# A graph network block on one core: places of a counting sort carried on in PSUM in place of column scans, padding spread over several rows, and the gather list turned by two groups

## What is computed

```
z    = concat([x[src], x[dst], edge_attr]) @ W.T + b          # per edge, 256 wide
z    = batch_norm(z, over all edges)
msg  = sigmoid(z[:, :H]) * softplus(z[:, H:])
agg  = zeros_like(x).at[src].add(msg)
x1   = layernorm(x + x + agg)
sums = segment_sum(x1[src], dst);  cnt = segment_sum(1, dst)
gain = tanh(norm(x1 - sums / max(cnt, 1)))
h    = x1 + 0.2 * (relu(x1 @ W1 + b1) @ W2 + b2) * gain
out  = layernorm(x1 + layernorm(h))
```

## Time and profile before

| what | value |
|---|---|
| time, median of 3 executions | 3955.68 us (3945.11 to 3955.88) |
| the profiled execution, span | 5481.6 us |
| stage 1, counting and source chain | 0 to 380 us of the profile |
| stage 1, list loop | 380 to 1749 us |
| stage 2 | 1749 to 3300 us |
| stage 3 | 3300 to 4249 us |
| stage 4 | 4249 to 5407 us |
| stage 5 | 5407 to 5482 us |

### The profile page before, as it was taken

The page is one execution under the profiler, slowest core; times in us unless marked ns, Lnnn a source line. Parts: engine busy times, 40 slices in busy tenths (PEclk is TensorE's granted clock), DMA queues, the critical chain, the costliest instruction groups (busy, mean ns, idle before and its releaser), DMA issues. The chain is left out here.

```text
span 5481.6 us, 84513 instructions
## 1 busy us (share of the span) xinstructions
PE 3436.3 (63%) x18854; PEld 2395.6 (44%) x18855; DVE 2979.6 (54%) x7781; ACT 2242.8 (41%) x6113; POOL 2626.3 (48%) x2634
## 2 busy tenths in 40 slices
PE   6745666666656888888888885661175555455542
PEld 2312222222223666666666664551165445445542
DVE  7975555555655333333333337971198555455547
ACT  1405555555654444444444448971197000000002
POOL 3775444444553555555555550077600544545542
PEclk8957777778877888888888887885587777777766
DMA  5322222122221666656666575463443221222213
GB/s 166 110 88 67 60 65 63 59 61 65 61 68 56 191 190 186 195 186 188 188 191 188 184 173 222 169 241 114 130 194 87 58 49 47 53 53 53 56 41 39
DMA packets 314711, 638.06 MB, mean 116 GB/s; under 512 B 54382, under 2 KB 188567, under 8 KB 306551
## 3 DMA queue, kind: packets, MB, share of 16 engines
q0 software_dynamic: 99440, 246.85, 16.9%
q1 hardware_dynamic: 172984, 266.76, 15.7%
q10 hardware_dynamic: 42192, 123.38, 6.1%
HBM read 424.53 MB, written 212.24 MB: 116 GB/s over the span
## 5 line engine op out<-in xcount | busy, mean ns | idle before, releaser
L367 POOL DMA_INDIRECT rec_d<-arena x830 | 887.8, 1070 | 815.8 <-issue 520.7
L853 POOL DMA_INDIRECT arena<-b_tab,arena x880 | 839.2, 954 | 730.4 <-DVE arena L874 405.8
L767 PE MATMUL psum<-arena 128*128 128x440 f16 x3360 | 776.5, 390 | 369.5 <-DVE arena L626 140.8
L626 DVE TENSOR_SCALAR arena<-iota_t,arena 128x880 f16<-128x880 f16 x840 | 516.1, 664 | 545.9 <-remote 320.5
L461 ACT ACTIVATE arena<-arena 128x128 f16<-128x128 f16 x1680 | 568.5, 388 | 469.9 <-remote 333.1
L767 PEld LDWEIGHTS psum<-arena 128*128 128x128 f16 x3360 | 344.2, 106 | 803.5 <-DVE arena L626 322.1
L1569 PE MATMUL psum<-arena,x_sb 128*128 128x129 f32 x2304 | 398.3, 347 | 454.2 <-DVE x_sb L1456 320.9
L964 PE MATMUL psum<-weT,arena 128*128 128x256 f32 x1760 | 627.6, 443 | 31.9 <-DVE arena L874 21.9
L1448 DVE TENSOR_TENSOR arena<-psum,arena 128x258 f32 x880 | 375.3, 426 | 476.9 <-remote 282.2
L1569 PEld LDWEIGHTS psum<-arena,x_sb 128*128 128x128 f32 x2304 | 375.7, 257 | 480.4 <-issue 192.3
L1255 POOL DMA_INDIRECT arena<-x_tab,arena x304 | 299.9, 987 | 556.1 <-DMA x_tab<-arena 295.9
(11 more groups left out here) (251 smaller groups left out, 5920.5 us busy)
## 6 DMA issues: line engine op xcount, KB each, us to landing
z_d<-arena ACTq DMA_DIRECT2D x220, 512.0 KB
arena<-z_d SPq DMA_DIRECT2D x44, 2560.0 KB
arena<-rec_d SPq DMA_DIRECT2D x220, 260.0 KB
arena<-in_edge_attr SPq DMA_DIRECT2D x83, 640.0 KB
arena<-early_d SPq DMA_DIRECT2D x34, 516.0 KB
arena<-b_tab,arena POOLq DMA_INDIRECT x880
rec_d<-arena POOLq DMA_INDIRECT x831
early_d<-arena POOLq DMA_DIRECT2D x9, 1032.0 KB
```

The lines of the kernel that those rows point to most:

```text
L367: nc.gpsimd.indirect_dma_start(rec_rows, bass.IndirectOffsetOnAxis(e_idx[:, s, k:k + 1], 0), e_buf[:, s, k, :], None).then_inc(s_es[s], 16)
L626: nc.vector.tensor_scalar(hot_tile[:, s, :].rearrange("p (a b) -> p a b", b=TILE_RUN), iota_t[:, :, 0:TILE_RUN], tile_f[:, bass.ds(t, 1)], ...
L767: last = nc.tensor.matmul(bank(4 + 2 * k + h)[:, 0:HALF], hot_lane[:, s, k, :], hot_tile[:, s, h * HALF:(h + 1) * HALF], start=start, stop ...
L853: nc.gpsimd.indirect_dma_start(bg[:, s, k, :], None, b_tab, bass.IndirectOffsetOnAxis(rec[:, s, k, H:H + 1].bitcast(I32), 0)).then_inc(s_b ...
```

## The change

There are three edits.

**Places carried on.** For each of the two chains, one bank of PSUM now holds, for every key and column, the place at which the next edge of that column goes. It starts from the counts (`chain_starts`: one scan, two more operations, once for each chain). In a step PE adds the ranks inside the column (`ranks`, one matmul with `tribig`), DVE reads the bank, and then PE adds the rest of the column's count (`move_on`: two matmuls, `restb` and `identb`), so that the bank is ready for the next step. The scans and the running sums of every step are gone. The destination's loop body now holds two batches.

**Padding over several rows.** The padding records' destination is `N_NODES` + (lane mod 16). In the second list an empty slot points to a row of its own lane (`PAD_ROW` + lane), 128 zeroed rows.

**List turned.** The second list is turned by `LAST_FIRST` = 2 groups (16 tiles): its last two groups come first. `EARLY` is 36. The first two groups are gathered at the start of stage 3 (when they are empty, for which the wait is on `s_end`), the other 34 as before. So there are 74 direct groups, 18 rounds and two direct groups behind them.

```diff
-EARLY, EARLY_BLOCKS, EARLY_TILES = 34, 16, 300
+EARLY, EARLY_BLOCKS, EARLY_TILES = 36, 16, 300
+LAST_FIRST = 2
+END_TILES = LAST_FIRST * G
...
-                def sum_columns(dest, hots):
-                    return nc.vector.tensor_tensor_scan(dest, not_first[:, 0:dest.shape[1]], hots, 0.0, ALU.mult, ALU.add)
+                def chain_starts(places, counted, n):
+
+                    upto, first = chain[:, 0, 0:n * G_IN], chain[:, 1, 0:n * G_IN]
+                    after(nc.vector.tensor_tensor_scan(upto, not_first[:, 0:n * G_IN], counted, 0.0, ALU.mult, ALU.add))
+                    after(nc.vector.tensor_tensor(first, upto, counted, ALU.subtract))
+                    after(nc.vector.scalar_tensor_tensor(by_col(places), tstart[:, 0:n].unsqueeze(2).broadcast_to([P, n, G_IN]), float(P), by_col(first),
+                                                         ALU.mult, ALU.add))
...
+                after(nc.vector.tensor_scalar(lane_row, lane, 15, None, ALU.bitwise_and))
+                after(nc.vector.tensor_scalar(pad_dst, lane_row, float(N_NODES), None, ALU.add))
...
                     if b + 2 < NB:
                         hot(hot_s[:, (b + 2) % 4, :], hi_s, b + 2).then_inc(s_hr, 1)
-                        dve.wait_ge(s_hr, b + 3)
-                        sum_columns(upto_s[:, (b + 2) % 3, :], hot_s[:, (b + 2) % 4, :]).then_inc(s_up, 1)
...
-                    if b + 3 < NB:
-                        run_src(b + 3)
                     dve.wait_ge(s_rg, b + 1)
-                    after(nc.vector.tensor_reduce(pos10, by_col(bank(b % 2)[:, 0:HB]).rearrange("p b c -> p c b"), op=ALU.max, axis=AX_X))
-                    nc.vector.tensor_scalar(p_i, pos10, -BIG, None, ALU.add).then_inc(s_rd, 1)
+                    nc.vector.tensor_reduce(pos10, by_col(CHAIN_S).rearrange("p b c -> p c b"), op=ALU.max, axis=AX_X).then_inc(s_rd, 1)
                     dve.wait_ge(s_rd, b + 1)
+                    after(nc.vector.tensor_scalar(p_i, pos10, -BIG, None, ALU.add))
...
-                def next_hot(b):
-                    nc.vector.tensor_tensor(run_d, run_d, by_col(upto_d)[:, :, G_IN - 1], ALU.add).then_inc(s_card, 1)
-                    hot(hot_d, hi_d, b).then_inc(s_hd, 1)
-                    dve.wait_ge(s_hd, b + 1)
-                    sum_columns(upto_d, hot_d).then_inc(s_upd, 1)
+                def next_hot(b, s):
+                    hot(hot_d[:, s, :], hi_d, b).then_inc(s_hd, 1)
...
-                after(nc.vector.tensor_scalar(l1_idx[:, 0:G * EARLY], l1_idx[:, 0:G * EARLY], early_key, None, ALU.add))
+                padded = l_words[:, 0:SLOTS]
+                after(nc.vector.tensor_scalar(padded[:, END_TILES:G * EARLY], l1_loc[:, END_TILES:G * EARLY], 0.0, early_key, ALU.is_gt, ALU.mult))
+                after(nc.vector.tensor_tensor(l1_idx[:, END_TILES:G * EARLY], l1_idx[:, END_TILES:G * EARLY], padded[:, END_TILES:G * EARLY], ALU.add))
+                after(nc.vector.tensor_scalar(padded, l1_loc[:], 0.0, pad_row, ALU.is_equal, ALU.mult))
+                after(nc.vector.tensor_tensor(l1_idx[:], l1_idx[:], padded, ALU.max))
...
+                def ranks(places, hots):
+
+                    return nc.tensor.matmul(places, tribig, hots, start=False, stop=False, skip_group_check=True)
+
+                def move_on(places, hots):
+
+                    nc.tensor.matmul(places, restb, hots, start=False, stop=False, skip_group_check=True)
+                    nc.tensor.matmul(places, identb[:], hots, start=False, stop=False, skip_group_check=True)
...
                     pe.wait_ge(s_hr, b + 1)
-                    pe.wait_ge(s_up, b + 1)
-                    if b >= 2:
-                        pe.wait_ge(s_rd, b - 1)
-                    ranks(bank(b % 2)[:, 0:HB], hot_s[:, b % 4, :], upto_s[:, b % 3, :])
+                    ranks(CHAIN_S, hot_s[:, b % 4, :]).then_inc(s_rg, 1)
                     if ab < BLOCKS:
                         less(ab, 0)
-                    pe.wait_ge(s_run, b + 1)
-                    before(bank(b % 2)[:, 0:HB], run_s[:, b % 4, :]).then_inc(s_rg, 1)
+                    pe.wait_ge(s_rd, b + 1)
+                    move_on(CHAIN_S, hot_s[:, b % 4, :])
...
                 for g in range(EARLY):
+                    if g == LAST_FIRST:
+                        pool.wait_ge(s_xs, ready)
+                        settle(pool, s_turn)
```

More of the change, by code:

```diff
@@ L222, in build @@
         hot_tile = tmp([HOTS, SLOTS], F16)
-        upto_s = tmp([3, HB], BF16)
+        tmp([3 * SLOTS - HOTS * SLOTS // 2], F32)
+        chain = arena[:, list_at:list_at + 2 * HK].rearrange("p (a n) -> p a n", a=2)
         l_words = arena[:, list_at:list_at + 3 * SLOTS]
@@ L267, in build @@
         COUNT_S, COUNT_D = bank(3)[:, 0:HB], bank(7)[:, 0:HK]
+        CHAIN_S, CHAIN_D = bank(0)[:, 0:HB], bank(1)[:, 0:HK]
         def by_col(v):
@@ L524, in tile_pairs @@
                 def tile_pairs():
-                    blocks_of(tile_id, blkf, KEYS)
+                    after(nc.vector.tensor_scalar(tile_in_list, tile_id, float(END_TILES), float(SLOTS), ALU.is_lt, ALU.mult))
+                    after(nc.vector.scalar_tensor_tensor(tile_in_list, tile_id, -float(END_TILES), tile_in_list, ALU.add, ALU.add))
+                    blocks_of(tile_in_list, blkf, KEYS)
                     after(nc.vector.tensor_scalar(blkf4, blkf, float(PAIRS), -float(PAIRS), ALU.is_ge, ALU.mult))
@@ L608, in _ @@
                 block_tiles(COUNT_D, KEYS)
-                nc.vector.tensor_copy(run_d, tstart).then_inc(s_card, 1)
-                hot(hot_d, hi_d, 0).then_inc(s_hd, 1)
-                dve.wait_ge(s_hd, 1)
-                sum_columns(upto_d, hot_d).then_inc(s_upd, 1)
+                chain_starts(CHAIN_D, COUNT_D, KEYS)
+                hot(hot_d[:, 0, :], hi_d, 0).then_inc(s_hd, 1)
                 tile_pairs()
@@ L654, in _ @@
                 places(1)
-                with dve.Fori(2, NB) as it:
-                    next_hot(it)
-                    dve.wait_ge(s_card, 5 * it)
-                    for k in range(G_IN):
-                        hots((it - 1) * G_IN + k, k % HOTS, it * G_IN + (k + 1 - HOTS - G_IN))
-                    places(it)
-                dve.wait_ge(s_card, 5 * NB)
+                with dve.Fori(1, NB // 2) as it:
+                    for h in range(2):
+                        b = 2 * it + h
+                        next_hot(b, h)
+                        dve.wait_ge(s_card, 4 * b)
+                        for k in range(G_IN):
+                            hots((b - 1) * G_IN + k, k % HOTS, b * G_IN + (k + 1 - HOTS - G_IN))
+                        places(b)
+                dve.wait_ge(s_card, 4 * NB)
                 for k in range(G_IN):
@@ L726, in _ @@
                     count_src(b + 4)
-                def ranks(region, hots, upto):
-                    nc.tensor.matmul(region, tribig, hots, start=True, stop=False, skip_group_check=True)
-                    nc.tensor.matmul(region, onesb, upto, start=False, stop=False, skip_group_check=True)
-                def before(region, run):
-                    return nc.tensor.matmul(region, onesh, run.unsqueeze(2).broadcast_to([P, run.shape[1], G_IN]),
-                                            start=False, stop=True, skip_group_check=True)
+                def ranks(places, hots):
[3 more added lines that the diff above has]
+                    nc.tensor.matmul(places, identb[:], hots, start=False, stop=False, skip_group_check=True)
                 for b in range(NB):
@@ L753, in _, with rank_dst @@
                     nc.tensor.matmul(COUNT_D, onesb, hot_c[:, b % 2, :], start=(b == 0), stop=(b == NB - 1)).then_inc(s_cd, 1)
-                def rank_dst(b):
+                def rank_dst(b, s):
+                    if not (isinstance(b, int) and b == 0):
+                        pe.wait_ge(s_card, 4 * b - 3)
+                        move_on(CHAIN_D, hot_d[:, 1 - s, :])
                     pe.wait_ge(s_hd, b + 1)
-                    pe.wait_ge(s_upd, b + 1)
-                    pe.wait_ge(s_card, 5 * b + 1)
-                    ranks(bank(0)[:, 0:HK], hot_d, upto_d)
-                    before(bank(0)[:, 0:HK], run_d).then_inc(s_rgd, 1)
+                    ranks(CHAIN_D, hot_d[:, s, :]).then_inc(s_rgd, 1)
                 def place(t1, s, start, stop):
@@ L769, in place @@
                     last.then_inc(s_list, 1)
-                rank_dst(0)
-                rank_dst(1)
+                rank_dst(0, 0)
+                rank_dst(1, 1)
                 pe.wait_ge(s_p[2], BLOCKS)
@@ L776, in _ @@
                     place(k + 1, k % HOTS, k == 0, False)
-                with pe.Fori(2, NB) as it:
-                    rank_dst(it)
-                    for k in range(G_IN):
-                        place((it - 1) * G_IN + (k + 1), k % HOTS, False, False)
+                with pe.Fori(1, NB // 2) as it:
+                    for h in range(2):
+                        b = 2 * it + h
+                        rank_dst(b, h)
```

(4 more changed lines are left out.)

106 lines of the change are left out of this document (60 added, 46 removed).

## The result

The changed kernel takes 3823.07 us (median of 4 runs, 3820.0 to 3823.89), the kernel before 3950.39 in the same comparison (4 runs, 3940.65 to 3955.88). The ratio is 0.9682, 95% interval 0.9663 to 0.9701: faster by 127 us or 3.2%, well outside the 0.3% that can't be told.

The account below looks back on a forecast made before the run. The prediction took POOL, with its indirect DMA calls, as the bound (ACT in stage 3). Stage 1 -51, padding -5, turned list -13 and loads +3 made -66 us: 3956 to 3890 us, range 3825 to 3944.

Parts of the forecast that it names:

- floors of 1200, 1100, 622, 770 and 75: Stages 1 to 5: least time in us at POOL's pace, for stage 3 ACT's busy time; sum 3767 us.
- slack of 189 us: Whole kernel: what the stages' floors leave of the timed run; the prediction fails if it lies in stage 3.
- some 100 calls x 0.18 = 18 us: Stage 1's scatter: POOL's calls get shorter by half the difference between 1.38 and 1.01 us, 18 us.
- priced at 37 us: Stage 1's scatter: if two-input scans cause the longer calls, their shortening gives up to 37 us in place of 18.
- Source chain -22: Stage 1, source chain: steps without a product fall from 3.30 to 2.60 us, those with one gain nothing; -22 us.
- List loop 37 to 105: Stage 1, list loop: ACT's wait for `places` goes in 84 batches, 37 us at least, 105 at most.
- Stage 1 in sum: -51 forecast: Stage 1: 55 us gained, the middle of lists alone (93) and scatter alone (18), less 4 for a longer tail.
- Rival 1: Whole kernel: POOL is the bound throughout, stage 1 gains only 14 us, the rounds nothing; 3940 us, chance 0.2.
- rival 2: Stage 1: the lists are the bound and gain up to 142 us; 3790 to 3865 us, chance 0.2.
- Rival 3: Source chain: the round through PSUM is slower, 5.9 us a step with a product, not 3.48; 3976 us, chance 0.07.
- Padding -5: End of stage 2: spreading z's 26 same-row padding gathers gives 5 us (0 to 22); other padding counted at nothing.
- Turned list -13, loads +3: Stage 4 loses sixteen gathers, two thirds of 20 us; at stage 3's start they delay z's first loads by 3 us.

Follow-up runs that it names:

- e0: The kernel before, unchanged, profiled once more on a chip of the usual level: 3946.02 us.
- e1: Kernel before with only the places carried on in PSUM; padding in one row, list not turned: 3859.77 us, ratio 0.9797 to the kernel before.
- e3: Changed kernel with the padding's spreading taken back (places and turned list stay): 3837.79 us, ratio 0.9741 to the kernel before.
- e2: Changed kernel with the turned list taken back (places and spread padding stay): 3831.47 us, ratio 0.9723 to the kernel before.
- e16: The kernel before, unchanged, profiled beside the changed kernel on a chip of the 5.5 ms level: 5557.30 us.

## Why the prediction was half right

**What bounds the kernel** was right: POOL, with floors of 1200, 1100, 622, 770 and 75. The changed kernel's stages are near them (1165, 1099, 755 for 592 direct gathers, 85), all but stage 3: from the last gather of z to the first direct one are 741 us in e0 and 714 in the changed kernel, against a floor of 622. So of the "slack of 189 us" some 119 lay in stage 3, which the prediction had named as one of the ways in which it would fail. That the profile's extra 1526 us are waits was right as well; that they fall on any run of a certain kind of chip, I did not see.

**The step that failed is the price of POOL's shorter calls, "some 100 calls x 0.18 = 18 us".** The thought behind it ("POOL's own work falls only where its calls get shorter") was right and it was the whole of stage 1. The runs showed 91 us in its place (e0 to e1), of which 58 moved the end of stage 1: 61 in the source chain and 30 in the list loop. Three sizes were wrong. The chain has 172 calls, not 100. Nearly all of the difference between 1.38 and 1.01 us went, not "half"; the mean hid that calls are of two kinds, 0.97 and 1.7 to 1.9 us. And the list loop was put at nothing, since I had taken its mean of 1.01 for the undisturbed length, which is 0.96. The rule of the Trainium skill, which I priced at 37 us and set aside since "rows show the two lengths side by side but not the cause", was the cause; with 172 calls its 0.37 us would have given 64. The range of a call's lengths in the trace would have shown it.

**Source chain -22:** its length came out so, from 292.8 (48.7 to 341.5) to 269.0 us (47.4 to 316.4). DVE's reads are 3.48 us apart with a product and 2.59 without one (1.9 to 2.1 for the first eight; the granted clock is 1.00 up to 250 us and 0.52 behind), against forecasts of 3.5 and 2.60, and DVE waits 99.0 us for `ranks`. But nothing waited for it: with the lists 23 us earlier, POOL still set the end.

**List loop 37 to 105:** from (1198.7 - 358.7) / 83 = 10.12 to (1139.4 - 336.1) / 83 = 9.68 us a batch, 37 us. That is my lower bound to the microsecond and for another reason: 30 calls go with four batches, and they became shorter. ACT waited 188.8 us for scatter slots in e0 and 131.7 in the changed kernel, and for `places` it waited only 12 us in all of e0's list loop and 2 in the changed kernel's, against 90 in the profile of the prediction, which is the slow chip's. So the 1.25 us of the earlier trace rows had been no price. Stage 1 in sum: -51 forecast, -56 measured, a right number out of a mixture of two bounds where there was one. Rival 1 (POOL throughout) had the mechanism and gave it 14 in place of 56. The measured time lies in rival 2's 3790 to 3865, but by luck: its 142 us from the lists did not happen. Rival 3's slow round did not happen at the 3.95 ms level; on the slower chips the chain did get 121 and 114 us longer, by late releases of DVE's read.

**Padding -5:** -28 timed when added to the places, -15 when added last (e3 to the changed kernel, two comparisons). In z it is 12 us. "Gathers there still keep up by themselves" was wrong: at the level of the timed runs 23 same-row gathers took 40 us, 1.74 each, while the others go at 1.25, and 26 x (1.74 - 1.25) = 13. That is the cost of a gather that the term had too low. In the earlier trace rows 23 calls to 40 us could be read, but beside 24 in the ordinary window, because the slow chip held those up too. The last 40 us of z, e1:

```profile
q0 software_dynamic: 986, 2.69, 72.1%
arena<-b_tab,arena POOLq DMA_INDIRECT x23
```

and the changed kernel:

```profile
q0 software_dynamic: 1540, 4.20, 37.1%
arena<-b_tab,arena POOLq DMA_INDIRECT x33
```

33 gathers in place of 23. The share of 37.1% is above my 26%, for there are more of them: 0.45 us each. "Leave padding in other tiles at nothing" missed ten more us: x1's padding is the last thing gathered, and the kernel's end waits for its transfers (tail 93.3 in e1, 83.6 in e2).

**Turned list -13, loads +3:** direct gathers went from 768.7 (e2) to 754.8 us, -14, and from 769.8 (e1) to 751.5, -18, so two thirds of 20 was about right as a number, and by luck. Less the surplus of their calls (10 and 16 us, 11 and 13 us) the direct gathers became 20.0 us shorter both times: POOL paces them throughout, and the changed kernel's one long call beside the 6.68 us operation hides a part of it. The sixteen gathers in front cost nothing (281.3 and 281.0 to early), where I had put 3. Not seen was that turning also takes x1's padding away from the end, 6.5 us where the padding isn't spread.

**Missing altogether:** the 18 us of stage 3, for which it stays open whether they are the change's, and 7 to 11 ns less for every undisturbed call.

## What to carry to other kernels

Where POOL's indirect DMA calls are the bound, list their lengths one by one. If the long ones lie beside DVE operations with two SBUF inputs, the cost is one of DVE's form of instruction, not of its time. Here moving the work to PE and PSUM took it away, and an idle one-input operation in its place did not bring it back. When the bound engine gets faster, look at once for the hand-made timing that fed it (here a fill after every fifth product): it was nearly level with the old pace and is late for the new one. Before a profile is used for what is full and what is not, hold its span against the timed runs; a view taken where everything waits hides exactly the small differences, such as 23 calls against 33.

## What was not expected of the hardware

- Chips differ. In three comparisons the kernel before took 3943 to 3968 us, in three others 5376 to 5557, with POOL's and DVE's instructions at the same lengths. What is added there are waits that the trace calls remote, e16:

```profile
ACT arena L921 <- remote: 661.5, 106, 19.4
DVE arena L880 <- remote: 545.8, 76, 13.5
```

  The mean granted TensorE clock is lower too (0.78 against 0.90). There the change is worth nothing or less (5576.09 against 5557.30 us). What those waits wait for no run here shows.
- Same-row gathers: 128 lanes on one row of z's table hold the 16 DMA engines for 72.1% of 40 us for 23 calls, 1.25 us each, against 0.45 for different rows.
- The undisturbed indirect calls of every changed kernel are shorter than in the kernel before, in stages whose code is the same (shortest gather of z: 942 to 945 ns against 949 at the 3.95 ms level, 940 to 943 against 947 to 951 on the slower chips). Over 880 of them 7 ns are 6 us, and z's gathers took 4.3 less in e1. The cause is not known.
- In "early" one call in three is longer than 1.03 us (e0: 100 of 272; changed kernel 86 of 272). The longest in e0 starts together with a two-input DVE operation of 6.68 us. It ends 3.2 us after it and not 0.8, and what holds it that much longer is not shown:

```profile
3051.88 6.68 DVE L1484 TENSOR_TENSOR arena<-arena 128x6272 f32<-128x6272 f32 x1
3052.03 9.74 POOL L1245 DMA_INDIRECT arena<-x_tab,l_idx  x1 [0.30 <-issue]
```
